# Layer norm of the last four batches on a turned x: rows through DRAM instead of transposes on TensorE

## The chip, the cores and the metric

The kernel runs on one NeuronCore of a Trainium2 chip. The metric is the device time of one execution in microseconds, the median of several runs. The engines are named as the profile names them: PE is TensorE's matmuls and PEld its weight loads, DVE is VectorE, ACT is ScalarE, POOL is GpSimd, SP is SyncE, which here issues DMAs only.

## The reference

Eight batches of 256 tokens with 256 features pass through two residual blocks. `ctx` has 120 rows of 256 per batch; the weights of the second block are ternary (-1, 0, 1) with a scale per output.

```python
def reference(x, ctx, w1_w, w1_s, w2_w, w2_s, h1_w, h1_s, h2_w, h2_s, w3_w, w3_s):
    n = layernorm(x)                                   # over the 256 features
    s = einsum('eth,efh->etf', n, ctx)
    x = x + einsum('etf,efh->eth', gelu_tanh(s) * s, ctx)
    n = layernorm(x)
    h = silu(tlin(n, w1_w, w1_s)) * tlin(n, w2_w, w2_s)     # 256 -> 1024
    h = gelu(tlin(h, h1_w, h1_s))                            # 1024 -> 1024
    h = gelu(tlin(h, h2_w, h2_s))                            # 1024 -> 1024
    return x + tlin(h, w3_w, w3_s)                           # 1024 -> 256
# tlin(x, w, s) = einsum('bsi,oi->bso', x, w) * s, layernorm without gain and bias, eps 1e-5
```

## The kernel before

Everything stays in float32 quality: each left operand of the large products is split into a rounded upper half (TH, half precision, written by ACT) and the rest (TL, written by VectorE), and TensorE multiplies both. The 1024x1024 layers are cut in 512x512 blocks and done with seven block products instead of eight (`ORDER`, `SUMS`, `PLAIN`), with the sums of blocks made on VectorE.

The work goes in two halves `c` of four batches, and in each half in tiles `t` of two batches (512 tokens). For each half: layer one of tile 2c (`layer1`), two block products, layer one of tile 2c+1, the other products of the first square layer (`late_products`), the second square layer (`square`, products s = 0 to 6), then layer four for its two tiles (`layer4_upper`, `layer4_lower`; half 1 first, then half 0), and `last` adds the result to x. The order on every engine is written out by hand; engines meet by semaphores, and each engine, SP too, does its list strictly in order.

The attention block of a batch is small and is tucked into the gaps of the large work: `stats` (mean and variance of x by VectorE into `mv`), `rstd` (POOL raises the variance to the power -0.5 into `rs`), `scale` (VectorE, line 894: xn = (x - mean) * power, two operations of 128 tokens each), `turn` (TensorE, line 1324: four transposes of 128x128 into a PSUM bank, `side(b)`), `copy_t` (ACT, line 612: the bank into `xt`), `score` (line 1335: two matmuls against ctx), `act_s` (gelu), `gate` (VectorE), `weigh` (line 1343), `resid` and the second layer norm, `turn(1, b)`, `first` and `second` into X, the operand of layer one. Batches 0 to 3 are done before and during the first layer one. Batches 4 and 5 are done at the end of the first half: VectorE scales them in `square(0)`, at s = 3 and s = 5; TensorE turns both after the first four products of layer four's half 1 (`attend4`) and scores them after the lower ones. Batches 6 and 7 are scaled, turned and scored inside `layer1(2)`.

Beside this runs a check of the weights' values: SP loads pieces of them into the spare buffers SL and Y, `xn[0]` and `xt` (`load_check`; each waits for the test before last), ACT takes the magnitude (`magnitude`, line 603) and VectorE tests (`test`, line 1036). Loads 7 and 8 are tested in `square(0)` at s = 5 and s = 6. POOL issues the weight loads (queue q0 in the profile), SP all others (queue q1).

In `square(0)` at s = 5 VectorE adds totals, tests, makes the low halves for product 6 (`lo`) and scales batch 5. At s = 6 it makes the totals of block (0, 0) (`total`, line 1030). On each of these waits ACT's gelu (line 714), on that ACT's rounded copy `hi4` (line 680), and on that layer four's first products on TensorE (line 1492) and VectorE's `lo4` (line 1000). Between the third copy and the fourth gelu stands the magnitude of load 8.

## Time and profile before

| | |
|---|---|
| median of 3 runs | 321.61 us (321.39 to 322.7) |
| profiled execution | 322.71 us, of which the span is 320.9 us |
| granted TensorE clock, every slice | 9 tenths or more of full speed; mean 1.0 |
| PE / DVE / ACT / POOL busy | 98% / 82% / 69% / 19% |
| the chain that ended last | PE 96% |
| queue q0 (POOL): packets, MB, share of 16 DMA engines | 21984, 52.43, 58.4% |
| queue q1 (SP): packets, MB, share | 9744, 22.11, 20.4% |

Busy time is the share of the span in which the engine had an instruction running. The chain is followed back from the last instruction, at each step to what released it; what stands in it sets the end. A row of a timeline gives the start in microseconds from the span's start, the duration of the merged instructions, the engine and the line, and in brackets how long the engine stood idle before and who released it. Rows named SPq or POOLq are the issuing of DMAs, not the transfer. A packet is one piece that a DMA engine moved.

### The profile page before, as it was taken

The page shows a single profiled execution, that of the slowest core. Times are in us where ns is not written, and L with a number is a line of the kernel's source. Part 1 is how long each engine was busy: PE and PEld are TensorE (multiplying, and loading weights), DVE is VectorE, ACT ScalarE, POOL GpSimd, SP SyncE. Part 2 cuts the span into 40 slices and gives each one's busy share as a digit, 9 for nine tenths or more (in the row PEclk, how much of TensorE's full clock was granted, in tenths as well). Part 3 has the DMA queues.
Part 4 walks back from the last instruction along what each step waited for, and adds up shares of the span by engine and source line. Part 5 has one row for each costly group of instructions (what it writes and reads, how often), then busy time and mean ns, then how long its engine had stood idle before and what let it go on. Part 6 is the DMA issues. An engine that isn't in the chain of part 4 may idle for free.

```text
span 320.9 us, 4928 instructions
## 1 busy us (share of the span) xinstructions
PE 313.8 (98%) x1624; PEld 226.9 (71%) x1624; DVE 264.2 (82%) x500; ACT 221.3 (69%) x372; POOL 59.6 (19%) x98
## 2 busy tenths in 40 slices
PE   7899999999999999999999999999999999999994
PEld 5799768774756657577898866876574756657693
DVE  4776996897996999998789494499899998998494
ACT  3657856781987857869825565978588975968740
POOL 5455010411120124114030003001121110220000
PEclk9999999999999999999999999999999999999999
DMA  7799999999999989998417055347599977877003
GB/s 205 253 173 270 207 262 319 315 393 400 321 340 419 303 294 254 334 270 187 133 66 262 2 196 194 137 129 261 198 275 293 394 254 293 203 189 198 0 29 111
DMA packets 31757, 74.90 MB, mean 233 GB/s; under 512 B 2160, under 2 KB 14192, under 8 KB 29296
## 3 DMA queue, kind: packets, MB, share of 16 engines
q0 software_dynamic: 21984, 52.43, 58.4%
q1 hardware_dynamic: 9744, 22.11, 20.4%
q8 instruction: 15, 0.25, 0.3%
q14 instruction: 14, 0.11, 0.1%
HBM read 71.39 MB, written 6.29 MB: 242 GB/s over the span
## 4 chain that ended last, share of the span: by engine, by line
PE 96%; DVE 1%; DMA 1%; POOL 0%; issue 0%; ACT 0%; DVEq 0%; POOLq 0%
PE P L1419 32%; PE P L1413 30%; PE P L1371 18%; PE P L1505 5%; PE P L1492 4%; PE P L1343 2%; PE P L1335 2%; PE P L1324 2%; DMA xs<-in_x 1%; PE P L1581 0%; POOL rs L474 0%; PE P L1588 0%; PE P L1574 0%; DVE st L900 0%; DVE hh L937 0%
## 5 line engine op out<-in xcount | busy, mean ns | idle before, releaser
L1419 PE MATMUL P<-TL,WR 128*128 128x512 f32 x448 | 107.4, 396 | 0.0
L1413 PE MATMUL P<-TH,WB 128*128 128x512 f16 x448 | 99.8, 379 | 0.0
L1419 PEld LDWEIGHTS P<-TL,WR 128*128 128x128 f32 x448 | 83.9, 188 | 18.6 <-DMA WR<-in_h 0.2
L673 ACT ACTIVATE TH<-H 128x512 f16<-128x512 f32 x112 | 67.9, 625 | 22.3 <-DVE H L986 14.0
L1413 PEld LDWEIGHTS P<-TH,WB 128*128 128x128 bf16 x448 | 42.4, 98 | 53.1 <-issue 4.5
L993 DVE TENSOR_TENSOR TL<-H,TH 128x512 fp32r<-128x512 f32 x112 | 73.2, 684 | 7.7 <-ACT TH L673 5.6
L1371 PE MATMUL P<-X,W 128*128 128x512 f32 (+1 forms) x320 | 62.5, 351 | 0.0
L1371 PEld LDWEIGHTS P<-X,W 128*128 128x128 f32 x320 | 51.7, 189 | 7.6
L986 DVE TENSOR_TENSOR H<-H 128x512 f32<-128x512 f32 x64 | 41.8, 683 | 0.0
L964 DVE SCALAR_TENSOR_TENSOR H<-P,sc,SLY 128x512 f32<-128x512 f32 (+1 forms) x40 | 25.3, 637 | 18.2 <-PE P L1371 11.0
L694 ACT ACTIVATE H<-P 128x512 f32<-128x512 f32 x48 | 28.5, 594 | 14.8 <-DMA blocks_h<-H 6.5
L662 ACT ACTIVATE SLY<-P,sc 128x512 f32<-128x512 f32 (+1 forms) x40 | 24.1, 603 | 18.4 <-PE P L1371 15.3
L714 ACT ACTIVATE H<-H,sc 128x512 f32<-128x512 f32 x40 | 27.4, 712 | 6.6 <-DVE H L1030 6.6
L1030 DVE TENSOR_TENSOR H<-P,H 128x512 f32<-128x512 f32 x40 | 25.6, 681 | 1.6 <-PE P L1413 1.3
L524 POOL DMA_DIRECT2D WB<-blocks_h x16 | 8.7, 546 | 97.2 <-PE P L1413 81.6
L1000 DVE SCALAR_TENSOR_TENSOR TL<-H,TH 128x512 fp32r<-128x512 f32 x32 | 20.6, 684 | 7.5 <-ACT TH L680 6.7
L1036 DVE SCALAR_TENSOR_TENSOR SLY<-SLY 128x1024 f32<-128x1024 f32 x14 | 17.0, 1218 | 3.0 <-ACT SLY L603 3.0
L680 ACT ACTIVATE TH<-H 128x512 f16<-128x512 f32 x32 | 18.0, 619 | 0.4 <-PE P L1413 0.4
L1505 PE MATMUL P<-WR,TL 128*128 128x256 f32 x128 | 18.3, 290 | 0.0
L469 POOL TENSOR_TENSOR rs<-mv,mhalf 128x2 f32<-128x2 f32 x14 | 11.4, 814 | 36.8 <-DVE mv L884 36.6
L603 ACT ACTIVATE SLY<-SLY 128x1024 f32<-128x1024 f32 x14 | 14.5, 1050 | 3.1 <-DMA SLY<-in_w 1.9
L714 ACT ACTIVATE H<-P,sc 128x512 f32<-128x512 f32 x24 | 15.5, 681 | 1.5 <-PE P L1413 1.5
(93 smaller groups left out, 257.1 us busy)
## 6 DMA issues: line engine op xcount, KB each, us to landing
WR<-blocks_h POOLq DMA_DIRECT2D x16, 1024.0 KB, 6.6
WR<-in_h POOLq DMA_DIRECT2D x11, 1024.0 KB, 9.4
WB<-blocks_h POOLq DMA_DIRECT2D x16, 512.0 KB, 5.5
WB<-in_h POOLq DMA_DIRECT2D x12, 512.0 KB, 8.1
H<-in_h POOLq DMA_DIRECT2D x8, 512.0 KB, 15.6
blocks_h<-H SPq DMA_DIRECT2D x4, 1024.0 KB, 8.9
SLY<-in_h SPq DMA_DIRECT2D x8, 512.0 KB, 5.0
SLY<-in_w SPq DMA_DIRECT2D x6, 512.0 KB, 8.1
```

The source lines that it names most:

```text
L662: eng.activation(SL[:, g % 2, at], bank1(t, 2 * m, p)[:, at], ACT.Silu, scale=sc[:, m:m + 1]).then_inc(s_sl, 1)
L673: eng.activation(TH[:, f % RING, :], operand(c, L, s, kk), ACT.Copy).then_inc(s_hi, 1)
L694: eng.activation(tile(target(c, L), to, m), bank(c, L, s, m)[:, :], ACT.Copy).then_inc(s_sn, 1)
L714: eng.activation(to, src, ACT.Gelu, scale=sc[:, col:col + 1]).then_inc(s_ge, 1)
L964: eng.scalar_tensor_tensor(out=source(t // 2, 0)[:, m, t % 2, at], in0=bank1(t, 2 * m + 1, p)[:, at], scalar=sc[:, 8 + m:9 + m], in1=SL[:, ...
L986: eng.tensor_tensor(tile(src, to, kk), tile(src, one, kk), tile(src, two, kk), ALU.subtract).then_inc(s_td, 1)
L993: eng.tensor_tensor(TL[:, f % RING, :], operand(c, L, s, kk), TH[:, f % RING, :], ALU.subtract).then_inc(s_lo, 1)
L1030: eng.tensor_tensor(to, bank(c, L, s, m)[:, :], other, ALU.add).then_inc(s_cd, 1)
L1371: out_ = eng.matmul(bank1(t, i, p)[:, at], w, X[:, t % 2, h, k, at], start=(k == 0 and h == 0), stop=(k == 1 and h == 1))
L1413: return eng.matmul(bank(c, L, s, m)[:, :], WB[r % WRING][:, at:at + 128], TH[:, fill(c, L, s, kk) % RING, :], start=(not lower_first and ...
L1419: return eng.matmul(bank(c, L, s, m)[:, :], WR[r % WRING][:, at:at + 128], TL[:, fill(c, L, s, kk) % RING, :], start=(lower_first and s in ...
L1505: out_ = eng.matmul(out_bank(c, half, j), TL[:, f % RING, j * 128:(j + 1) * 128], WR[r % WRING][:, k * D:(k + 1) * D], start=False, stop=( ...
```

## The change

For batches 4 to 7 the first layer norm is done on x that lies turned (features on partitions). The host hands the kernel a second input, `x_turned`; SP loads a batch of it into `xt` (256 KB, `load_turned`). The mean and the power of two batches go from `mv` and `rs`, where a token is a partition, to an internal DRAM tensor `rows` (`rows_out`: two DMAs, each of 128 partitions with 4 single floats, written 4 bytes at a time). From there they come back for each batch as two rows of 256 floats on all 128 partitions, into `xn[0]` (`rows_in`, 256 KB). VectorE then does (x - mean) in `center` and times the power in `spread_out`, both in place in `xt`, 128x512 values each. TensorE's `turn(0, b)` and ACT's `copy_t` for these batches are gone, and VectorE's `scale(0, b)`. The mathematics is the same. `score` now holds the wait for the bank that `turn` held.

```diff
+        rows = nc.dram_tensor("rows_x", [2, NB, 2, 128], f32, kind="Internal").ap()
...
+            def load_turned(b):
+
+                eng.wait_ge(s_s, b - 1)
+                eng.dma_start(xt[:, b % 2, :, :], x_turned[:, b, :, :]).then_inc(s_xT[b], 16)
+
+            def rows_out(b):
+
+                eng.wait_ge(s_mv[0], b + 2)
+                eng.dma_start(rows[0, b:b + 2, :, :].rearrange("b j p -> p (b j)"),
+                              mv[:, 0, b % 4:b % 4 + 2, :, 0].rearrange("p b j -> p (b j)"),
+                              allow_slow_non_contiguous=True).then_inc(s_row, 16)
+                eng.wait_ge(s_rs[0], b + 2)
+                eng.dma_start(rows[1, b:b + 2, :, :].rearrange("b j p -> p (b j)"),
+                              rs[:, 0, b % 4:b % 4 + 2, :].rearrange("p b j -> p (b j)"),
+                              allow_slow_non_contiguous=True).then_inc(s_row, 16)
+
+            def rows_in(b):
+                if b < 6:
+                    eng.wait_ge(s_tr[0], b - 1)
+                else:
+                    eng.wait_ge(s_xt, b - 1)
+                eng.dma_start(xn[0][:, b % 2, :, :],
+                              rows[:, b:b + 1, :, :].rearrange("v b j p -> b v (j p)").broadcast_to([128, 2, TB])).then_inc(s_bc[b], 16)
...
-            for i in range(2, 9):
+            for i in range(2, 4):
                 load_check(i)
+            load_turned(4)
+            load_turned(5)
+            for i in range(4, 8):
+                load_check(i)
+            rows_out(4)
+            eng.wait_ge(s_row, 32)
+            rows_in(4)
+            rows_in(5)
+            load_check(8)
+            rows_out(6)
+            load_turned(6)
+            load_turned(7)
+            eng.wait_ge(s_row, 64)
+            rows_in(6)
+            rows_in(7)
...
-                    if t == 2 and m in (3, 4):
-                        copy_t(3 + m)
...
-                    if i >= 2:
-                        if c == 0:
-                            copy_t(2 + i)
-                        else:
-                            gelu(c, 1, (1, 0), i)
+                    if i >= 2 and c == 1:
+                        gelu(c, 1, (1, 0), i)
...
+            def center(b):
+
+                eng.wait_ge(s_xT[b], 16)
+                eng.wait_ge(s_bc[b], 16)
+                eng.tensor_tensor(xt[:, b % 2, :, :], xt[:, b % 2, :, :], xn[0][:, b % 2, 0:1, :].broadcast_to([128, 2, TB]),
+                                  ALU.subtract).then_inc(s_xm, 1)
+
+            def spread_out(b):
+                eng.wait_ge(s_xm, b - 3)
+                eng.tensor_tensor(xt[:, b % 2, :, :], xt[:, b % 2, :, :], xn[0][:, b % 2, 1:2, :].broadcast_to([128, 2, TB]),
+                                  ALU.mult).then_inc(s_xt, 1)
...
-                    if c == 0 and s == 3:
-                        scale(0, 4)
...
                     if c == 0 and s == 5:
-                        scale(0, 5)
+                        for b in (4, 5):
+                            center(b)
+                            spread_out(b)
...
-                    if t == 2 and m < 2:
-                        scale(0, 6 + m)
+                    if t == 2 and m < 4:
+                        (center, spread_out)[m % 2](6 + m // 2)
...
-                if norm == 0 and b in (4, 5):
-
-                    gelu_done(eng, 0, 1, b, 0)
...
             def score(b):
                 eng.wait_ge(s_cf[b // 2], 16)
+                if b in (4, 5):
+
+                    gelu_done(eng, 0, 1, b, 0)
...
-                if t == 2 and i in (6, 8):
-                    turn(0, 3 + i // 2)
...
-                if (half, k, upper) == (1, 3, True):
-                    turn(0, 4)
-                    turn(0, 5)
```

How the rows of instructions stand now is shown at two places; the line numbers of the changed kernel differ from those before. On SP, from the load of the last scales (s3b) to the first stores of results (out), before:

```order
L421 DMA s3b<-in_s 128x256
L386 DMA SLY<-in_w 128x1024 [waits s_fl] x2
L388 DMA SLY<-in_w 128x1024 [waits s_fl] x2
L391 DMA SLY<-in_h 128x1024 [waits s_fl] x3
L427 DMA out<-xs 128x512 [waits s_y2] x4
```

and now, with check load 8 on its own behind the rows:

```order
L449 DMA s3b<-in_s 128x256
L414 DMA SLY<-in_w 128x1024 [waits s_fl] x2
L381 DMA xt<-in_x_turned 128x512 [waits s_s] x2
L416 DMA SLY<-in_w 128x1024 [waits s_fl] x2
L419 DMA SLY<-in_h 128x1024 [waits s_fl] x2
L386 DMA rows_x<-mv 128x4x1 [waits s_mv1]
L390 DMA rows_x<-rs 128x4x1 [waits s_rs1]
L399 DMA xn<-rows_x 128x2x256 [waits s_tr1,s_row]
L399 DMA xn<-rows_x 128x2x256 [waits s_tr1]
L419 DMA SLY<-in_h 128x1024 [waits s_fl]
```

The writing of the rows stands behind check load 7 (the second of L419 x2), their reading behind the landing of both writes, and check load 8 behind the reading.

On VectorE, the end of s = 5 and the beginning of s = 6 of the second square layer, from the test of load 7 (SLY) over the low halves (TL) to the totals (H<-P), before:

```order
L1036 SCALAR_TENSOR_TENSOR SLY,fl<-SLY 128x1024 [waits s_ab]
L993 TENSOR_TENSOR TL<-H1,TH 128x512 [waits s_tf,s_hi] x4
L894 TENSOR_SCALAR xn0<-xs,mv,rs 128x256 [waits s_rs1,s_mv1,s_tr1]
L894 TENSOR_SCALAR xn0<-xs,mv,rs 128x256
L1030 TENSOR_TENSOR H0<-P6,H0 128x512 [waits s_sn,s_p]
L1030 TENSOR_TENSOR H0<-P7,H0 128x512 [waits s_sn,s_p]
L1000 SCALAR_TENSOR_TENSOR TL<-H0,TH 128x512 [waits s_tf,s_hi]
```

and now, with the same names:

```order
L1086 SCALAR_TENSOR_TENSOR SLY,fl<-SLY 128x1024 [waits s_ab]
L1043 TENSOR_TENSOR TL<-H1,TH 128x512 [waits s_tf,s_hi] x4
L939 TENSOR_TENSOR xt<-xt,xn0 128x512 [waits s_bc4,s_xT4]
L944 TENSOR_TENSOR xt<-xt,xn0 128x512 [waits s_xm]
L939 TENSOR_TENSOR xt<-xt,xn0 128x512 [waits s_bc5,s_xT5]
L944 TENSOR_TENSOR xt<-xt,xn0 128x512 [waits s_xm]
L1080 TENSOR_TENSOR H0<-P6,H0 128x512 [waits s_sn,s_p]
L1080 TENSOR_TENSOR H0<-P7,H0 128x512 [waits s_sn,s_p]
L1050 SCALAR_TENSOR_TENSOR TL<-H0,TH 128x512 [waits s_tf,s_hi]
```

Four operations that wait for DMAs (s_bc, s_xT) stand where two scalings stood, ahead of the totals.

## Rows read from the trace of the kernel before

**Rows 1.** The page, part 1: busy us, share of the span, instructions.

```profile
PE 313.8 (98%) x1624; PEld 226.9 (71%) x1624; DVE 264.2 (82%) x500; ACT 221.3 (69%) x372; POOL 59.6 (19%) x98
```

**Rows 2.** The chain of waits in order of time: start us, us, what.

```profile
137.08 7.28 PE P L1419 x32
...
147.83 1.75 PE P L1492 x16
149.58 0.87 PE P L1324 x8
...
174.11 0.44 PE P L1324 x4
...
176.41 0.44 PE P L1324 x4
```

**Rows 3.** DVE's timeline around 141 us: start, us, what, idle before and releaser.

```profile
137.98 2.49 DVE L993 TENSOR_TENSOR TL<-H,TH 128x512 fp32r<-128x512 f32 x4
140.39 0.72 DVE L894 TENSOR_SCALAR xn<-xs,mv,rs 128x256 f32<-128x256 f32 x2
141.04 1.28 DVE L1030 TENSOR_TENSOR H<-P,H 128x512 f32<-128x512 f32 x2
143.03 0.69 DVE L1000 SCALAR_TENSOR_TENSOR TL<-H,TH 128x512 fp32r<-128x512 f32 x1 [0.71 <-ACT TH L680]
```

**Rows 4.** ACT's timeline in the same stretch.

```profile
141.75 0.72 ACT L714 ACTIVATE H<-H,sc 128x512 f32<-128x512 f32 x1 [2.46 <-DVE H L1030]
...
145.50 1.04 ACT L603 ACTIVATE SLY<-SLY 128x1024 f32<-128x1024 f32 x1
...
147.06 0.61 ACT L680 ACTIVATE TH<-H 128x512 f16<-128x512 f32 x1
```

**Rows 5.** PE's timeline, first products of layer four.

```profile
147.67 1.91 PE L1492 MATMUL P<-WB,TH 128*128 128x256 bf16 x16
```

**Rows 6.** SP's timeline: two loads of check data, of one window each.

```profile
126.86 0.33 SPq L391 DMA_DIRECT2D SLY<-in_h  x1
...
131.22 0.33 SPq L391 DMA_DIRECT2D SLY<-in_h  x1
```

**Rows 7.** POOL's timeline: the power of batch 5.

```profile
120.27 1.04 POOL L469 TENSOR_TENSOR rs<-mv,mhalf 128x2 f32<-128x2 f32 x1 [5.96 <-DVE mv L884]
```

**Rows 8.** DMA queues, 127 to 130 us: packets, MB, share of 16 engines.

```profile
q0 software_dynamic: 593, 0.87, 123.0%
```

**Rows 9.** The same, 130.2 to 133 us.

```profile
q0 software_dynamic: 299, 0.41, 63.6%
q1 hardware_dynamic: 142, 0.52, 50.3%
```

**Rows 10.** The same, 134.3 to 136.6 us.

```profile
q1 hardware_dynamic: 141, 0.52, 57.6%
```

**Rows 11.** The same, 2.5 to 3 us and then 7 to 7.5 us.

```profile
q1 hardware_dynamic: 143, 0.13, 102.5%
...
q1 hardware_dynamic: 97, 0.04, 29.1%
```

**Rows 12.** DMA issues over the whole run: count, KB each, median us to landing.

```profile
xs<-in_x SPq DMA_DIRECT2D x2, 128.0 KB, 2.2
out<-xs SPq DMA_DIRECT2D x4, 128.0 KB, 2.6
```

**Rows 13.** DVE's timeline: a pair in which the second waits for the first.

```profile
167.23 0.68 DVE L1163 SCALAR_TENSOR_TENSOR SLY<-P,s3b 128x512 f32<-128x512 f32 x1
167.94 0.69 DVE L1168 TENSOR_TENSOR xs<-SLY,xs 128x512 f32<-128x512 f32 x1
```

**Rows 14.** DMA issues between 126.5 and 134 us: a weight load.

```profile
WR<-in_h POOLq DMA_DIRECT2D x1, 1024.0 KB, 10.6
```

**Rows 15.** DVE's timeline in the third layer-one stretch.

```profile
173.19 0.73 DVE L894 TENSOR_SCALAR xn<-xs,mv,rs 128x256 f32<-128x256 f32 x2
...
182.36 0.75 DVE L964 SCALAR_TENSOR_TENSOR H<-P,sc,SLY 128x512 f32<-128x512 f32 x1 [1.35 <-PE P L1371]
```

More of the change, by code:

```diff
@@ L48, with xattn_ffn @@
 SPIN = (13, 1)
-def xattn_ffn(nc, x, ctx_tok, ctx_feat, w12, h1, h2, w3, cols, s3, out):
+def xattn_ffn(nc, x, x_turned, ctx_tok, ctx_feat, w12, h1, h2, w3, cols, s3, out):
     f32, f32r, u16, i32 = mybir.dt.float32, mybir.dt.float32r, mybir.dt.uint16, mybir.dt.int32
@@ L162, in xattn_ffn @@
         s_m4, s_y, s_y2, s_out = sem("s_m4"), sem("s_y"), sem("s_y2"), sem("s_out")
+        s_xT = {b: sem(f"s_xT{b}") for b in range(4, NB)}
+        s_bc = {b: sem(f"s_bc{b}") for b in range(4, NB)}
+        s_row, s_xm = sem("s_row"), sem("s_xm")
         s_ab, s_fl, s_fp, s_ft = sem("s_ab"), sem("s_fl"), sem("s_fp"), sem("s_ft")
@@ L1690, in _ @@
                     out_.then_inc(g_m3, 1)
-_INS = ["x", "ctx_tok", "ctx_feat", "w12", "h1", "h2", "w3", "cols", "s3"]
+_INS = ["x", "x_turned", "ctx_tok", "ctx_feat", "w12", "h1", "h2", "w3", "cols", "s3"]
 def kernel(x, ctx_1024, L0_ffn_w1_w, L0_ffn_w1_s, L0_ffn_w2_w, L0_ffn_w2_s, L0_ffn_h1_w, L0_ffn_h1_s,
@@ L1714 @@
         "x": np.asarray(x).reshape(NB * TB, D),
+        "x_turned": np.asarray(x).reshape(NB, 128, 2, 2, 128).transpose(4, 0, 3, 2, 1).reshape(128, NB, 2, TB),
         "ctx_tok": np.pad(c.transpose(1, 0, 2), ((0, 128 - S), (0, 0), (0, 0))),
```

## The prediction

> **What bounds the kernel now.** I read the page first, then the chain of waits, then the timelines of the stretch where the change lands, then the DMA queues there. TensorE is busy 313.8 of 320.9 us [rows 1], and the chain that ended last is TensorE almost from end to end. So only two things move the time: work taken off TensorE, and a wait put in front of it. The transposes that the change removes stand in that chain three times: one piece of 8 for batches 4 and 5, and two of 4 for batches 6 and 7 [rows 2]. The granted clock is full in every slice of the page, so it takes no part in the sum.
>
> **What goes from TensorE.** 16 transposes in pieces of 0.87, 0.44 and 0.44 us [rows 2]: 1.75 us. The chain counts by how much each piece holds up the next matmul, so this is the term. This is the whole possible gain, 0.54% of the run.
>
> **What goes from and comes to the other engines.** ACT loses four copies out of the PSUM bank, all in places where it is not the last to be ready. VectorE loses four pairs of scalings of about 0.72 us (one is at 140.39 in [rows 3]) and gets eight operations on 128x512 values. The nearest row is a 128x512 tensor_tensor: four in a row start 0.60 us apart (137.98 to 140.39) [rows 3], and one that waits for the one before it starts 0.71 us after it [rows 13]. A batch therefore costs 1.31 us. Batches 6 and 7 pay this between the gates of the third layer-one stretch, where VectorE has its scaling at 173.19 and sits idle 1.35 us before 182.36 [rows 15]. The extra there is 2 x (1.31 - 0.72) = 1.2 us, which this idle time swallows; without that cover it would cost up to 1.2.
>
> **The place that decides: VectorE before layer four.** Before, the scaling of batch 5 ran at 140.39 and the totals of the last block began at 141.04 [rows 3]. Everything behind is a tight relay: gelu on ACT at 141.75, a magnitude of 1.04 us between, the fourth rounded copy at 147.06 lasting 0.61 [rows 4]. VectorE itself waits 0.71 us for ACT in it at 143.03 [rows 3]. So the fourth copy is ready 147.67 - 141.04 = 6.63 us after the totals begin. TensorE starts layer four at 147.67 [rows 5] and takes 1.75 us for 16 products of four copies [rows 2], so it wants the fourth copy at 147.67 + 3/4 x 1.75 = 148.98. The totals may then begin at 142.35 and no later; every later microsecond is a microsecond of TensorE, because all engines in this relay are in order.
>
> In the changed order VectorE has center(4), spread_out(4), center(5), spread_out(5) ahead of the totals. With all data there they start at 140.39, 141.10, 141.70 and 142.41, and the totals at 143.01: 0.66 us of stall even in the best case. If the rows of batch 5 land at T, the totals begin at T + 1.31 and the stall is T - 141.04. The changed order queues behind the waiting instruction all of VectorE: totals, the low halves for layer four, the test of data 8, the statistics of batch 7; ACT and TensorE wait for the first two.
>
> **When do the rows land?** SP is in order too. It issues the check load 7 at 126.86 [rows 6] and only then rows_out(4). The power of batch 5 is ready at 121.31 [rows 7], so values are no limit, the place in SP's queue is. I follow the queue:
>
> The check load issued at 126.86 moves nothing before 130.2: from 127 to 130 only POOL's queue q0 has packets [rows 8]. The next one, issued at 131.22 [rows 6], moves from 134.3 [rows 10]. So an SP transfer begins 3.1 to 3.3 us after its issue while POOL loads weights. The first is through at 133.0 (142 packets in [rows 9]: one packet for each 4 KB row of a partition, 128, and the completions).
>
> Writing the rows: two DMAs of 128 partitions x 4 single floats. Packets here go one per contiguous piece, so I count 1024 packets, 64 on each of 16 engines. No row shows a 4-byte packet. From below, the smallest packets that do show (97, on average 0.4 KB, 29.1% of 0.5 us) [rows 11] take 0.291 x 16 x 0.5 / 97 = 24 ns: 1.5 us. From above, each also waits for a packet of POOL's, 1.23 x 16 x 3 / 593 = 100 ns [rows 8]: 64 x 0.124 = 7.9 us. In [rows 9] the two queues did run mixed, so neither end is excluded; I take 5.0, near the middle: 138.0. A write lands 0.4 us later than a load of that size (2.6 against 2.2) [rows 12]; with SP's wake-up I take 0.7: 138.7.
>
> The Trainium skill (DMA: Bandwidth & Descriptors, Rules for kernel authors) says that a strided last dimension is lowered to one descriptor per element. The count of rows above does not rest on it, but it speaks against this edit: a packet per partition instead would make the writes 64 / 4 = 16 packets an engine, at most 2.0 us, and T some 3 us earlier. No run so far shows a strided write of this kind.
>
> Reading them back: two loads of 256 KB as 512 packets of 1 KB. They begin 3.2 us after issue as above: 141.9. A 1 KB packet takes 1.025 x 16 x 0.5 / 143 = 57 ns [rows 11]: 32 x 57 = 1.8 us alone, 32 x 157 = 5.0 us with a POOL packet each; I take 3.4: 145.3, and 0.5 for the completion: T = 145.8. Ends: all low, and the load starting as in a quiet stretch, 133.0 + 1.5 + 0.4 + 2.2 [rows 12] + 1.4 for the 384 packets beyond 128 = 138.5, which is in time; all high, 133.0 + 7.9 + 0.7 + 3.3 + 5.0 + 0.5 = 150.4.
>
> **Sum.** Stall 145.8 - 141.0 = 4.8; transposes -1.75; net +3.0 us. The profiled execution took 322.71 us, 320.9 of it the span and 1.8 around it; it would become 325.7. It was 1.1 above the median of 321.61, which becomes 324.6, my forecast. By the ends of T: 0.66 - 1.75 = -1.1 (320.5) and 9.4 - 1.75 = +7.6 (329.2).
>
> **Edits at nothing.** The turned x of batches 4 and 5 is issued after check 3, some 40 us ahead of its use; those of 6 and 7 and their rows, free to start some 5 us after layer four's first products at 147.67 [rows 5], have until 173 [rows 15], 20 us where the chain above needs 19 with a check load at its head (126.9 to 145.8); that is the thinnest cover of the four, and each microsecond over it would stop VectorE between two gates. Check load 8 now goes behind the rows, needs the 2.8 us of [rows 9] after T, and its magnitude stands 4.5 us after the totals begin (145.50 against 141.04) [rows 3, 4], T + 5.8: covered, and if not, it would stop ACT ahead of the fourth copy, microsecond for microsecond. The weight load that POOL issued near 126.8 landed after 10.6 us [rows 14], near 137.5, and is used half-way through the 32 products of 137.08 [rows 2], at 140.7; small packets mixed with its tail may push it 1 to 2 us: covered.
>
> **Rivals.** (1) Pure gain: the relay has slack I do not see and the rows are early; 321.61 - 1.75 = 319.9. For it: TensorE alone is the bound [rows 1]. Against it: 0.66 us of added VectorE work in a relay with 1.3 us of room, and SP's queue. Chance 0.07. (2) The rows land in time (T below 141.7), the gain shrinks by 0.66: 320.5, no change that can be measured. It needs the low end of both packet prices and no 3 us delay. Chance 0.18. (3) The forecast's mechanism with a price far above: the float writes go at the pace that q1's packets had in [rows 9], 142 in 2.8 us, 51 per us, so 1024 take 20 us; then T is 153 + 9.5 = 162.5, the stall 21, the time 341. It ends slower as well; 0.08. (4) The wait on the rows in place of the transposes, as summed: slower from T = 144.4 on, where the stall exceeds 1.75 + 1.6. This is my forecast, 0.67, of which 0.07 falls under that point; its own range is 322.4 to 329.2.
>
> **Chances.** A change of 0.5%, 1.6 us, is about what a measurement of this kernel can tell from none. Faster 0.07; same 0.18 + 0.07 = 0.25; slower 0.60 + 0.08 = 0.68. The range 320.2 to 331 leaves out the pure gain and the crawl, 0.15 in all, and a little of each neighbour.
>
> **What the profile after would show.** Right: no transposes between the 16 products of layer four and the next ones; VectorE idle for several microseconds before the first center, released by DMA; the totals starting at 143 to 149; TensorE idle in its first layer-four products, waiting for ACT's copy; q1 with about a thousand packets under 512 B near 133 to 139. Wrong: VectorE's center at 140.4 without idle time, or many fewer packets (the floats are merged), or the transposes of layer four worth more than 0.87 us. A second stall at the scores of batches 6 and 7 would break the part on cover.

## The result and the profile after

| | before | changed |
|---|---|---|
| median | 322.01 us (321.39 to 322.86, 6 runs) | 353.24 us (352.44 to 354.91, 6 runs) |
| profiled execution, its span | 322.71, 320.9 us | 354.44, 352.6 us |
| mean granted clock | 1.0 | 0.959 |

The ratio is 1.0975 (95% interval 1.0954 to 1.0997): 9.7% slower. The direction and the place were forecast; the size (+3.0 us) was short by a factor of ten. Of the versions below, the one with the writes alone was profiled in a slow execution (336.31 us; the three fast ones took 329.74, 329.82 and 330.82), so its time is read from those three and its trace only for where TensorE stops.

Three more rows of the kernel before: its DMA counts, then the groups of the lower products and of layer four's upper products (busy, mean ns | idle before).

```profile
DMA packets 31757, 74.90 MB, mean 233 GB/s; under 512 B 2160, under 2 KB 14192, under 8 KB 29296
...
L1419 PE MATMUL P<-TL,WR 128*128 128x512 f32 x448 | 107.4, 396 | 0.0
...
L1492 PE MATMUL P<-WB,TH 128*128 128x256 bf16 x128 | 15.9, 273 | 0.0
```

The page of the changed kernel: busy time by engine, then the granted TensorE clock by slice, the DMA counts and queues, and the same two groups of instructions (busy, mean ns | idle before, who ended it).

```profile
PE 321.9 (91%) x1608; PEld 231.0 (66%) x1608; DVE 267.1 (76%) x500; ACT 219.6 (62%) x368; POOL 59.3 (17%) x98
...
PEclk9999999999999999787599699999999999999998
...
DMA packets 35533, 77.01 MB, mean 218 GB/s; under 512 B 4400, under 2 KB 17456, under 8 KB 33072
...
q1 hardware_dynamic: 13520, 24.21, 26.9%
...
L1469 PE MATMUL P<-TL,WR 128*128 128x512 f32 x448 | 109.3, 400 | 8.6 <-DMA WR<-in_h 8.5
...
L1542 PE MATMUL P<-WB,TH 128*128 128x256 bf16 x128 | 18.1, 291 | 9.5 <-ACT TH L723 9.4
```

Against [rows 1] TensorE does 16 instructions fewer, is busy 8.1 us longer and is idle 23.6 us longer. Three things are to be seen. The clock row has slices at 5 to 8 tenths, where before every slice had 9. The lower products (L1469) wait 8.5 us for a weight load and layer four (L1542) 9.4 us for ACT's copies; both groups had no idle time before. And q1 has 13520 - 9744 = 3776 packets more: 2048 single floats, 1024 pieces of 1 KB of rows, 512 pieces of the turned x, and 16 completions for each of 12 DMAs. Of those, 2240 are under 512 bytes (4400 against 2160), the floats and the completions. The floats are not merged.

TensorE's timeline in the changed kernel, only its stops from 140 us on:

```profile
149.89 5.28 PE L1469 MATMUL P<-TL,WR 128*128 128x512 f32 x16 [8.54 <-DMA WR<-in_h]
...
166.54 2.12 PE L1542 MATMUL P<-WB,TH 128*128 128x256 bf16 x8 [7.91 <-ACT TH L723]
169.10 1.04 PE L1542 MATMUL P<-WB,TH 128*128 128x256 bf16 x4 [0.44 <-ACT TH L723]
171.18 1.03 PE L1542 MATMUL P<-WB,TH 128*128 128x256 bf16 x4 [1.04 <-ACT TH L723]
...
189.95 0.65 PE L1371 MATMUL P<-ident,xn 128*128 128x128 f32 x3 [1.20 <-issue]
195.30 1.23 PE L1371 MATMUL P<-ident,xn 128*128 128x128 f32 x5 [4.70 <-issue]
```

SP's timeline (what it issues; a gap is a wait) and below it VectorE's before layer four:

```profile
127.14 0.33 SPq L419 DMA_DIRECT2D SLY<-in_h  x1
127.51 0.44 SPq L386 DMA_DIRECT2D rows_x<-mv  x1
127.99 0.58 SPq L390 DMA_DIRECT2D rows_x<-rs  x1
150.82 1.39 SPq L399 DMA_DIRECT2D xn<-rows_x  x2
...
175.10 0.36 SPq L390 DMA_DIRECT2D rows_x<-rs  x1
...
195.21 1.08 SPq L399 DMA_DIRECT2D xn<-rows_x  x2
```

```profile
160.71 0.69 DVE L939 TENSOR_TENSOR xt<-xt,xn 128x512 f32<-128x512 f32 x1 [20.78 <-DMA xn<-rows_x]
...
163.15 0.69 DVE L939 TENSOR_TENSOR xt<-xt,xn 128x512 f32<-128x512 f32 x1 [1.02 <-DMA xn<-rows_x]
...
164.48 1.28 DVE L1080 TENSOR_TENSOR H<-P,H 128x512 f32<-128x512 f32 x2
```

The totals that began at 141.04 [rows 3] begin at 164.48, because 4 KB of rows took 22.8 us from the second write's issue (127.99) to the issue of the read (150.82), and the read another 10 to 12. The second pair of writes, which starts while POOL's queue is silent, takes 20.1 us as well (175.10 to 195.21).

Answers of the DMA view (packets, MB, share of 16 engines): q1 from 174 to 177 us, q0 from 141 to 151 us, q0 in the same stretch of the version without writes (below), q1 from 181 to 194 us; then the weight load that POOL issued between 126.5 and 134 us (KB, us to landing).

```profile
q1 hardware_dynamic: 1056, 0.00, 16.8%
```

```profile
q0 software_dynamic: 41, 0.17, 85.0%
```

```profile
q0 software_dynamic: 1339, 2.74, 100.9%
```

```profile
q1 hardware_dynamic: 92, 0.18, 101.2%
```

```profile
WR<-in_h POOLq DMA_DIRECT2D x1, 1024.0 KB, 22.4
```

The first row is the surprise. The 1024 floats of the second pair (and 32 completions) are off the engines within 3 us, at 0.168 x 16 x 3 / 1056 = 7.6 ns each, but their DMAs are complete only at 195.2. The first pair, which shares the engines with POOL's loads, is slower there: of its 1056 packets 44 are moved before 133 us and the other 1012 between 133 and 141, with engine time of 0.742 x 16 x 8 / 1012 = 94 ns each. Its DMAs are complete at 150.8, still 10 us after the last packet.

In that time whatever else is in flight crawls. From 141 to 151 us 4 KB packets of POOL's take 0.85 x 16 x 10 / 41 = 3.3 us each: 41 in 10 us, where the version without writes has 1339. In the second stretch SP's loads of the turned x still have 144 packets from 178 to 180 us, and then 92 in the 13 us from 181 to 194. The weight load of [rows 14] goes from 10.6 to 22.4 us.

Sum for the profiled execution: weight load 8.54, ACT's copies 7.91 + 0.44 + 1.04 = 9.39, the two stops before the transposes of the second layer norm 5.90: 23.8 of idle time. TensorE's busy time without the 1.75 us of transposes would be 312.05; it is 321.9, so slower instructions cost 9.85 (8.8 if the 313.1 us of the version without writes, whose clock is 1.0, are the measure). 23.8 + 9.85 - 1.75 = 31.9, against 31.7 of span. The slower instructions stand behind the stops. The windows show it (us; busy and count of PE, PEld, DVE, ACT, POOL; granted clock, DMA share, GB/s):

```profile
137.00:141.00 4.00, 4.00 (x20) 3.10 (x17) 2.92 (x6) 2.03 (x4) 0.75 (x1) 1.00 1.96 47
141.00:150.00 9.00, 0.47 (x3) 0.11 (x1) 0.00 (x0) 0.00 (x0) 0.75 (x1) 0.77 0.85 16
150.00:158.00 8.00, 8.00 (x30) 5.19 (x31) 0.00 (x0) 0.00 (x0) 0.00 (x0) 0.83 0.86 208
...
166.00:178.00 12.00, 9.91 (x43) 7.38 (x44) 8.75 (x17) 10.98 (x19) 1.05 (x1) 0.56 0.50 123
...
195.00:204.00 9.00, 8.70 (x38) 7.90 (x38) 7.36 (x12) 3.97 (x6) 1.12 (x2) 0.69 0.39 95
```

The clock is 1.00 until TensorE stops at 141. It is 0.83 from 150 to 158, behind the first stop, and 0.56 from 166 to 178, behind the second: over those 12 us on average near the lower of its two levels (1.2 of 2.4 GHz). Behind the third, from 195 to 204, it is 0.69.

### The profile page after: what moved, and what is told of

It is laid out like the page before. It is cut to its first block, busy times and chain, and to the rows that moved or that the text cites. A ratio compares the mean times of both kernels' runs of the same rounds, so it can differ in the third digit from the quotient of the medians.

```text
span 352.6 us, 4898 instructions
## 1 busy us (share of the span) xinstructions
PE 321.9 (91%) x1608; PEld 231.0 (66%) x1608; DVE 267.1 (76%) x500; ACT 219.6 (62%) x368; POOL 59.3 (17%) x98
## 3 DMA queue, kind: packets, MB, share of 16 engines
q1 hardware_dynamic: 13520, 24.21, 26.9%
## 4 chain that ended last, share of the span: by engine, by line
PE 74%; DMA 12%; issue 4%; ACT 4%; DVE 4%; SPq 0%; DVEq 0%; ACTq 0%
PE P L1469 21%; PE P L1463 20%; PE P L1421 17%; DMA rows_x<-rs 6%; PE P L1555 5%; PE P L1542 4%; DMA xn<-rows_x 3%; DMA SLY<-in_w 2%; PE P L1385 2%; PE P L1393 2%; DVE H L1036 2%; ACT TH L716 2%; PE P L1371 2%; ACT SLY L646 1%; PE P L1564 1%
## 5 line engine op out<-in xcount | busy, mean ns | idle before, releaser
L1469 PE MATMUL P<-TL,WR 128*128 128x512 f32 x448 | 109.3, 400 | 8.6 <-DMA WR<-in_h 8.5
L1469 PEld LDWEIGHTS P<-TL,WR 128*128 128x128 f32 x448 | 84.8, 190 | 28.2 <-DMA WR<-in_h 9.4
L716 ACT ACTIVATE TH<-H 128x512 f16<-128x512 f32 x112 | 67.9, 624 | 20.1 <-DVE H L1036 13.7
L1542 PE MATMUL P<-WB,TH 128*128 128x256 bf16 x128 | 18.1, 291 | 9.5 <-ACT TH L723 9.4
L1555 PE MATMUL P<-WR,TL 128*128 128x256 f32 x128 | 21.5, 325 | 0.0
L1542 PEld LDWEIGHTS P<-WB,TH 128*128 128x128 f16 x128 | 12.0, 102 | 13.6 <-issue 8.4
L1555 PEld LDWEIGHTS P<-WR,TL 128*128 128x128 f32 x128 | 19.2, 225 | 0.2
L939 DVE TENSOR_TENSOR xt<-xt,xn 128x512 f32<-128x512 f32 x4 | 2.7, 687 | 21.8 <-DMA xn<-rows_x 21.8
```

Of the source, the lines that this page charges most:

```text
L716: eng.activation(TH[:, f % RING, :], operand(c, L, s, kk), ACT.Copy).then_inc(s_hi, 1)
L1469: return eng.matmul(bank(c, L, s, m)[:, :], WR[r % WRING][:, at:at + 128], TL[:, fill(c, L, s, kk) % RING, :], start=(lower_first and s in ...
L1542: out_ = eng.matmul(out_bank(c, half, j), TH[:, f % RING, j * 128:(j + 1) * 128], WB[r % WRING][:, k * D:(k + 1) * D], start=(k == 0 and ( ...
L1555: out_ = eng.matmul(out_bank(c, half, j), TL[:, f % RING, j * 128:(j + 1) * 128], WR[r % WRING][:, k * D:(k + 1) * D], start=False, stop=( ...
```

## The experiments

The kernel before ran beside every group: 321.95, 321.79, 321.73 and 321.76 us median. Theory W is that the single-float writes are the loss, by the wait for them and by what they do to other transfers.

**1. Nothing is written** (e1_no_write). The rows are loaded from x, in the same pieces.

```diff
-            rows_out(4)
-            eng.wait_ge(s_row, 32)
...
-            rows_out(6)
...
-            eng.wait_ge(s_row, 64)
...
-   rows[:, b:b + 1, :, :].rearrange("v b j p -> b v (j p)").broadcast_to([128, 2, TB])
+   x[2 * b:2 * b + 2, :].rearrange("(b v) p -> b v p", b=1).broadcast_to([128, 2, TB])
```

> The changed kernel without the writes of mean and power to DRAM: the two rows come back from two rows of the input x, so the first layer norm of batches 4 to 7 uses wrong numbers. Theory W (the single-float writes are the cost: they finish about 22 us after their issue and hold up all other transfers meanwhile): without them no wait on the rows, no late weight load and no stall later; time near 321, at most 1.5 us either side of the kernel before. Rival R (the broadcast reads of the same two rows are a cost of their own: 12 us from issue to landing in the changed kernel): VectorE waits for them before its first center until 140 to 146 us, time 322 to 327.

320.24 us (320.02 to 321.46), ratio 0.9948 (0.9932 to 0.9964), clock 1.0. VectorE, no wait:

```profile
139.74 0.69 DVE L935 TENSOR_TENSOR xt<-xt,xn 128x512 f32<-128x512 f32 x1
...
142.40 1.28 DVE L1076 TENSOR_TENSOR H<-P,H 128x512 f32<-128x512 f32 x2
```

So turned loads, read-back, VectorE's eight operations and the missing transposes together are a gain of 1.7 us. All of the loss hangs on the writes and on the waits for them; rival R (the broadcast reads cost by themselves) falls. It also corrects a term: center begins at 139.74, not at 140.39, since the scaling of batch 4, 0.65 us at s = 3, is gone too, and TensorE does not wait at layer four.

**2. The writes alone** (e2_write_only). The kernel before, transposes and all, with the four writes on SP and nobody waiting for them until the end.

```diff
-            for i in range(2, 9):
-                load_check(i)
+            for i in range(2, 8):
+                load_check(i)
+            rows_out(4)
+            load_check(8)
+            rows_out(6)
```

> The kernel before, with its transposes, plus only the four single-float writes at the places where the changed kernel has them on SP; nobody waits for them before the end. Theory W, with writes that hold up other transfers: the weight load for the last product of the second square layer comes about 8.5 us late, the clock is lower for a while (1.5 to 3 us), and the turning for the second layer norm stops for 5 to 6 us; time 335 to 339. Rival Q (the writes only take long by themselves, and all of the cost is the waiting for them in SP and VectorE): time 322 to 323.

329.82 us (329.74 to 330.82), ratio 1.0245 (1.0212 to 1.0279). TensorE's first stop:

```profile
149.24 3.35 PE L1436 MATMUL P<-TL,WR 128*128 128x512 f32 x7 [8.17 <-DMA WR<-in_h]
```

Writes that nobody waits for cost 7.9 us, and the trace shows through what: another engine's weight load. So about a quarter of the 31 us is clogging alone. Rival Q (322 to 323) falls, but theory W's own range for this run, 335 to 339, was 5 us too high: the stop of 5 to 6 us at the second layer norm did not come. TensorE does these transposes at 175.49 without a stop marked "issue", though the DMA engines then move only 48 GB/s (166 to 178 us). What is left of the 31 us is the wait for the rows, the second pair's stretch in the changed order, and the clock.

**3. Each float in 512 bytes of its own** (e3_spread). The same 1024 writes of 4 bytes per pair, read back from x.

```diff
-        rows = nc.dram_tensor("rows_x", [2, NB, 2, 128], f32, kind="Internal").ap()
+        rows = nc.dram_tensor("rows_x", [2, NB, 2, 128, 128], f32, kind="Internal").ap()
...
-                eng.dma_start(rows[0, b:b + 2, :, :].rearrange("b j p -> p (b j)"),
+                eng.dma_start(rows[0, b:b + 2, :, :, 0].rearrange("b j p -> p (b j)"),
```

> The changed kernel with each float written to its own 512 bytes of DRAM (1024 writes as before, over 512 KB instead of 4 KB), and the rows read back from two rows of the input x, so the numbers are wrong. If the writes are slow because they all fall into the same few lines of DRAM and queue there: they finish within 3 to 6 us, and the time is 321 to 326. If each single-float write has its price wherever it goes: they finish about 22 us after issue as in the changed kernel, time 348 to 354 (a little less if the read back from x is quicker).

326.96 us (326.86 to 329.6), ratio 1.0173 (1.0109 to 1.0238). SP's and VectorE's timelines:

```profile
127.25 0.43 SPq L386 DMA_DIRECT2D rows_x<-mv  x1
...
136.51 0.96 SPq L399 DMA_DIRECT2D xn<-in_x  x2
```

```profile
144.54 0.69 DVE L939 TENSOR_TENSOR xt<-xt,xn 128x512 f32<-128x512 f32 x1 [4.87 <-DMA xn<-in_x]
```

9.3 us instead of 23.3 from the first write's issue to the read, no late weight load (9.2 us), a wait of 4.87 us. That is somewhat more than the 3 to 6 us and the 321 to 326 us expected. The number and size of the writes are those of the changed kernel; what makes the crawl is that they lie close together. This version behaves as I had forecast for the changed one.

**4. Half of the floats** (e4_half, partitions 0 to 63, `mv[0:64, ...]` and `rs[0:64, ...]`, read from x), and later **the means alone** (e8_means_only, without the second DMA of `rows_out`).

> The changed kernel with only the floats of partitions 0 to 63 written (512 instead of 1024 for a pair of batches, still four DMAs); the other tokens' mean and power are wrong. If the price is per write: the first pair is done about 9 to 11 us earlier, near 140 us, and VectorE's stall before center shrinks from 20.8 us to about 11; with the weight load less late as well the time is 334 to 343. If the price is per DMA and not per write: no change, 352 to 354.

341.61 us (339.76 to 341.89), ratio 1.0586 (1.0535 to 1.0636). SP:

```profile
127.42 0.69 SPq L386 DMA_DIRECT2D rows_x<-mv  x1
...
149.84 1.34 SPq L399 DMA_DIRECT2D xn<-in_x  x2
...
171.85 0.58 SPq L390 DMA_DIRECT2D rows_x<-rs  x1
...
186.09 0.80 SPq L399 DMA_DIRECT2D xn<-in_x  x2
```

> The changed kernel without the write of the power: 512 floats per pair of batches instead of 1024, still dense, 16 in each 64 bytes; rows read from x, so the values are wrong. Theory N (price per write): 10 us of crawl after about 3 us, rows_in issued near 140, center of batch 4 near 149, stall about 8, total 330 to 335 us. Theory D64 (price by depth, pieces served side by side): the crawl stays near 20 us, rows_in at 148 to 150, total 340 to 350, as where half the partitions were written (341.61).

332.13 us (331.37 to 332.4), ratio 1.0311 (1.0289 to 1.0333), rows_in at 141.58, center of batch 4 at 150.25 after 10.35 us of waiting. Both leave 512 floats with 16 in each 64 bytes, and they differ: 14.2 and 9.4 us from the last write's issue to the read in the second pair. With half the partitions the total lies in the expected 334 to 343, but not for the expected reason: the first pair was to be done 9 to 11 us earlier, and the read leaves at 149.84 against 150.82. The means alone come out as theory N (a price for each write) has it. The price is neither one for a float nor one for the depth of a piece alone.

**5. How close is too close** (e5_own64, e9_own16, e11_own8, e10_by_partition). As 3 with 64, 16 and 8 bytes for each float; in the last the 8 floats of a partition stand together without gaps, and 128 partitions in a row.

```diff
-        rows = nc.dram_tensor("rows_x", [2, NB, 2, 128], f32, kind="Internal").ap()
+        rows = nc.dram_tensor("rows_x", [2, NB, 2, 128, 16], f32, kind="Internal").ap()   # own64; 4, 2: own16, own8
+        rows = nc.dram_tensor("rows_x", [NB // 2, 128, 4, 2], f32, kind="Internal").ap()  # by_partition
```

> The changed kernel with each float of mean and power written into 64 bytes of its own (1024 writes of 4 bytes as before, 8 in each 512 bytes instead of 128); the rows that are read back are taken from x, so the values are wrong, the bytes and places of the reading are as before. Theory D64 (what costs is the number of writes that fall into one piece of 64 bytes, 16 in the changed kernel, 1 here): like the run with 512 bytes of its own, writes over 8 to 10 us after issue, rows read at 136 to 138, total 326 to 328 us. Theory D512 (the same with pieces of 512 bytes, 128 there, 8 here, price in proportion to the depth): 20 x 8 / 128 = 1.3 us more than with 512 bytes of its own, 327 to 329, hardly to be told apart. Theory F (only a stride of at least 512 bytes helps, since each smaller write reads and rewrites a piece shared with others, one after another): still a crawl of 10 us or more, 340 us and over.

> The same with each float in 16 bytes of its own: 1024 writes of 4 bytes, 4 in each 64 bytes, 32 in each 512 bytes. Theory D64, price in proportion to the depth: 20 x 4 / 16 = 5 us of writing beyond the spread case's own, rows read near 138 to 141, total 328 to 333. Theory D512: 20 x 32 / 128 = 5 us, the same. Theory N (every write that is not alone in its piece costs the same, about 20 ns): 20 us again, writes done near 150, total near 350.

> The changed kernel with each float in 8 bytes of its own: 1024 writes of 4 bytes, 8 in each 64 bytes, from 8 neighbouring partitions (16 in the changed kernel, 4 with 16 bytes each). What is read back comes from x, so the values are wrong. Theory D, in proportion from 4 writes (10.5 us from issue to rows_in) to 16 (22.8): about 14.6, rows_in near 142, total 332 to 338. Theory S, if an engine serves 8 neighbouring partitions and so owns its 64 bytes: still 10 to 11 us, total 328 to 330. If S holds with another division among the engines, the crawl comes back in part and this run can't tell it from D; then the run with the floats by partition decides.

> The changed kernel with the same 1024 writes of 4 bytes into the same 4 KB, without gaps in the end, but the 8 floats of a partition stand together in 32 bytes instead of 512 bytes apart (each still written by itself; what is read back comes from x, so the values are wrong). Each 64 bytes get 16 writes as in the changed kernel, but from 2 partitions instead of 16. Theory D (it is the number of writes into one piece of memory that costs): a crawl of 20 us, rows_in issued near 150, total 340 to 350. Theory S (it is that many partitions, and so several DMA engines, write into the same piece at once): rows_in issued near 138, as with 16 bytes for each float (138.36), total 327 to 331.

All of 3 to 5 side by side. "First" is the time from the first write's issue to the read's issue in the first pair, "second" from the last write's issue to the read's in the second pair, where POOL's queue is silent; a value with "up to" is one where SP reached the read no earlier for another reason.

| version | floats per pair | in each 64 bytes | first | second | median (ratio, interval) |
|---|---|---|---|---|---|
| changed | 1024 | 16 | 23.3 | 20.1 | 353.24 (1.0975) |
| half the partitions | 512 | 16 | 22.4 | 14.2 | 341.61 (1.0586) |
| means alone | 512 | 16 | 14.1 | 9.4 | 332.13 (1.0311) |
| by partition | 1024 | 16, of 2 partitions, 8 by each DMA | 14.1 | 7.2 | 332.43 (1.0362, 1.0323 to 1.0401) |
| 8 bytes each | 1024 | 8 | 14.0 | 6.7 | 332.05 (1.0313, 1.0292 to 1.0335) |
| 16 bytes each | 1024 | 4 | 11.0 | up to 3.2 | 329.26 (1.0221, 1.0192 to 1.0249) |
| 64 bytes each | 1024 | 1 | 9.9 | up to 2.9 | 326.63 (1.013, 1.0104 to 1.0157) |
| 512 bytes each | 1024 | 1 | 9.3 | up to 3.1 | 326.96 (1.0173) |

Two rows of SP's timeline in the by-partition version, behind its 7.2:

```profile
163.84 0.52 SPq L390 DMA_DIRECT2D rows_x<-rs  x1
...
171.01 0.80 SPq L399 DMA_DIRECT2D xn<-in_x  x2
```

The price falls with the density: 20 us, 7 us, and with 16 bytes each a rest that the totals still show against 64 bytes (329.26 to 326.63, intervals apart; the interval of 512 bytes each overlaps both). 64 bytes each are as good as 512. Theory F (only 512 bytes help) is refuted. Theory N (every write alike) fits the means alone (332.13, in its range) and is refuted by 16 bytes each. Theory D64 (the depth of a piece alone, pieces served side by side) is refuted by the means alone: half the writes at the same depth take half the time. Theory S (many partitions in one piece) fails too: by it the by-partition version would be as quick as 16 bytes each (327 to 331), and 8 bytes each would take 328 to 330.

The by-partition version does not refute a price by density. Its 332.43 us lie in neither expected range, but its 16 floats in each 64 bytes come from two DMAs, 8 by each, while in the changed kernel one DMA writes all 16. Counted for each DMA it has the density of 8 bytes each, and it costs the same: 7.2 against 6.7 us, 332.43 against 332.05. That they come from 2 partitions there and from 8 here makes no difference. So these runs show that the number of writes counts and that their density within one DMA counts, more than in proportion (from 16 to 8 the 20.1 us fall to 6.7). The size of the piece is not shown: theory D512 expected 327 to 329 for 64 bytes each and can't be told from D64. Why half the partitions cost more than half the values is open as well; nobody tested how many DMA engines write into one piece. The second-pair times are from one profile each.

**6. The same dense writes, asked for earlier** (e13_floats_early).

```diff
-                    if c == 0 and s in (2, 3):
-                        stats(0, 2 + s)
+                    if c == 0 and s in (1, 2):
+                        stats(0, 3 + s)
...
-            for i in range(4, 8):
+            for i in range(4, 7):
                 load_check(i)
             rows_out(4)
+            load_check(7)
```

> The changed kernel with its single-float writes for batches 4 and 5 asked for one product earlier: statistics one product earlier, both writes behind check load 6 (issued near 120.3) and ahead of check load 7. Nothing is left out and the writes are the same 1024 dense ones. It tells what of the loss is the place in the order and what the writes themselves. Theory W (the writes clog whatever is in flight, wherever they stand): rows written only at 141 to 144 (20 to 22 us after issue), rows_in there, center of batch 4 at 146 to 150, check load 7 landing in the crawl, near 144 instead of 133, so ACT's magnitude of data 7 waits some 10 us and the lower products of the fifth block with it; the weight loads issued at 121 to 127 late too. Total 340 to 356 us, no clear gain over the changed kernel (353.24). Rival P (the place was the trouble: asked for early, the rows are there in time for 139.8 and the rest is covered): 325 to 335, about the cost of clogging alone (330.32).

346.68 us (345.57 to 347.66), ratio 1.0755 (1.0708 to 1.0802). SP, ACT and TensorE:

```profile
120.91 0.44 SPq L386 DMA_DIRECT2D rows_x<-mv  x1
...
127.23 0.34 SPq L419 DMA_DIRECT2D SLY<-in_h  x1
148.61 1.08 SPq L399 DMA_DIRECT2D xn<-rows_x  x2
```

```profile
150.57 1.06 ACT L647 ACTIVATE SLY<-SLY 128x1024 f32<-128x1024 f32 x1 [18.61 <-DMA SLY<-in_h]
```

```profile
154.88 6.22 PE L1470 MATMUL P<-TL,WR 128*128 128x512 f32 x16 [7.66 <-DMA WR<-in_h]
```

Asked for 6.6 us earlier, the rows are there 2.2 us earlier (the read leaves at 148.6, where 141 to 144 was expected), and check load 7, which had landed before the crawl, is now caught in it and stops ACT for 18.6 us. The place in the queue is not what was wrong: theory W holds (340 to 356), rival P (325 to 335) falls.

**7. A version without single floats** (e7_rows_turned, then e12_rows_early). Mean, variance and power of batches 4 to 7 share a 128x32 piece; VectorE turns it in 32x32 blocks, and a pair's rows leave as 32 pieces of 128 bytes. The second version makes the statistics one product earlier. Both compute the whole reference.

```diff
+            def turn_stats(k):
+                eng.wait_ge(s_rs[0], 6 + 2 * k)
+                eng.transpose(sT[:, k, :], sA[:, :]).then_inc(s_sT, 1)
...
+            def rows_out(b):
+                k = b // 2 - 2
+                eng.wait_ge(s_sT, k + 1)
+                for i in range(4):
+                    eng.dma_start(rows[k].rearrange("v b j p -> (v b j) p")[:, 32 * i:32 * i + 32],
+                                  sT[32 * i + 16 * k:32 * i + 16 * k + 16:2, k, :]).then_inc(s_row, 16)
...
-            for i in range(4, 8):
+            for i in range(4, 7):
                 load_check(i)
             rows_out(4)
+            load_check(7)
-            eng.wait_ge(s_row, 32)
+            eng.wait_ge(s_row, 64)
```

> A version meant to beat both: mean and power of batches 4 to 7 lie in one 128x32 piece, VectorE turns it in 32x32 blocks (two operations of some 0.1 us), and a pair's rows go out as 32 pieces of 128 bytes (4 DMAs of 8) instead of 1024 single floats; the writes are issued right behind the turning, ahead of check load 7. Nothing is left out. Theory W (the single floats alone were the loss): rows written by 131, read back by 137 to 138, center of batch 4 at about 139.8 without a wait, all as in the run without writes: 320.2 to 321.0 us, ratio 0.995 to 0.997 to the kernel before. Rival Q (the queue on SP still brings the rows late, the loads wait for POOL's packets): rows at 141 to 144, a stall of 1 to 4 us, 321.5 to 325. Rival M (any write from SBUF of less than 512 bytes clogs as before): over 330.

321.16 us (320.73 to 322.27), ratio 0.998 (0.9959 to 1.0001), just above theory W's 320.2 to 321.0; rival M (over 330) falls. ACT waits longer for check load 7, and VectorE is late for the totals:

```profile
134.64 1.06 ACT L653 ACTIVATE SLY<-SLY 128x1024 f32<-128x1024 f32 x1 [2.85 <-DMA SLY<-in_h]
```

```profile
142.92 1.28 DVE L1092 TENSOR_TENSOR H<-P,H 128x512 f32<-128x512 f32 x2
```

> The version with the rows turned on VectorE, with the statistics of batches 4 and 5 one product earlier and the turning at the place where the statistics of batch 5 stood (about 119.3). Its four writes leave SP behind check load 6 and are done before 126.9, check load 7 goes out at 126.9 instead of 128.4, and the rows are asked for right behind it. Nothing is left out. Theory L (the version before lost 0.5 us because four DMA issues held check load 7 up by 1.5 us, ACT's magnitude waited 0.87 longer, and the totals before layer four began at 142.92, 0.57 after the latest time of 142.35): ACT's magnitude back at 133.8, center of batch 4 at 139.8, totals at 142.5, no wait at layer four, span 318.4 to 318.6, time 320.2 to 320.7, ratio 0.994 to 0.997. Rival (any DMA work of the rows costs in another place, such as POOL's weight loads): 321.0 or more, as the version before (321.16).

320.26 us (320.13 to 321.55), ratio 0.9962 (0.9946 to 0.9978), as expected: a gain of 0.4%, small but with its interval clear of 1, over the kernel before. SP, and VectorE without a wait:

```profile
120.66 2.70 SPq L394 DMA_DIRECT2D rows_x<-sT  x4
127.06 0.34 SPq L422 DMA_DIRECT2D SLY<-in_h  x1
128.00 0.90 SPq L402 DMA_DIRECT2D xn<-rows_x  x2
```

```profile
120.18 0.20 DVE L945 STREAM_TRANSPOSE sT<-sA 128x32 f32<-128x32 f32 x1
...
139.77 0.68 DVE L951 TENSOR_TENSOR xt<-xt,xn 128x512 f32<-128x512 f32 x1
...
142.42 1.28 DVE L1092 TENSOR_TENSOR H<-P,H 128x512 f32<-128x512 f32 x2
```

The same bytes, 4 KB per pair, in 32 pieces instead of 1024, and the gain of the missing transposes is there: 1.2 us by the ratio, 1.5 by the medians.

## Why the prediction was wrong in size

**The writes, the step that failed.** The text priced 1024 floats as packets, "24 ns" from below and "64 x 0.124 = 7.9 us" from above, and took 5.0 us, from 133.0 to 138.0. As packets the first pair's took 8 us (133 to 141), the upper end; the second pair's, alone on the engines, took 7.6 ns each, below the lower end. But the DMA is complete 20.1 to 22.8 us after its issue, 10 to 19 us after the last packet. The forecast had 0.7 us for that part. It took this from a write of 128 KB [rows 12], and both packet prices from other transfers, none of which writes single floats side by side. With the floats 512 bytes apart the forecast's own numbers nearly hold: read issued at 136.5 (forecast 138.7), layer four's stops 4.2 us in sum (forecast 4.8), a time of 326.96 (forecast 324.6). The rest of that difference is in TensorE's busy time, 315.5 us against the 312.05 that the forecast implies, at a mean clock of 0.99.

**The rival that had it.** "The float writes go at the pace ... 51 per us, so 1024 take 20 us" gave T = 162.5 and 341 us, at 0.08. Batch 5's rows were used at 163.15: T was right to 0.7 us, by luck: the floats did not go at that pace, the first pair's left the engines in 8 us and the second's in 3. Its time was 12 us short, because it too counted the wait alone.

**Edits at nothing, the second failure.** The weight load of [rows 14], "may push it 1 to 2 us: covered", landed after 22.4 us instead of 10.6 and stopped TensorE for 8.54; in the writes-alone version the same stop is 8.17. A slow transfer was priced by who waits for it, never by what else it slows. For batches 6 and 7 the text gave "20 us where the chain above needs 19": VectorE never waited for those rows (the two waits in its group are those of batches 4 and 5). But their writes fall into the stretch of 176 to 195, and there TensorE stops 1.20 and 4.70 us, marked "issue". The stop is 5.9 us in the changed kernel, 2.1 with the writes asked for earlier, 1.2 (0.9 and 0.3) with half the partitions, none in the versions with a crawl under 10 us, and none with the writes alone, where the same dense writes are in flight. Late loading of instructions, whose queue q8 has 15 packets in the page after, could be the cause, but no run took that alone. The cause of these 5.9 us stays open.

**The clock.** "It takes no part in the sum" was true of before and fell with the stops: 9.85 us of slower instructions. None of my cases had a price for it, though all but the pure gain had a stall.

**What held.** The queue on SP: check load 7 landed 6.3 us after its issue at 127.14, at 133.4 (forecast 133.0). One packet for each float: in the Trainium skill, DMA: Bandwidth & Descriptors, Rules for kernel authors, a strided last dimension becomes one descriptor per element; the 2048 extra packets agree. The same page (Specifications) says that transfers under 512 bytes are read-modify-writes in the DMA engine. By that alone floats at 64 or at 512 bytes each should be as bad as dense ones, since each is still written 4 bytes at a time; they cost 326.63 and 326.96 against 353.24 us, so here the rule doesn't tell the cases apart, the density does. The transposes: 1.75 us forecast, 1.7 measured without the writes. The relay from totals to layer four: the latest start was put at 142.35; totals at 142.40 and 142.42 give no wait, those at 142.92 one of 0.4 us on TensorE. The 0.66 us of stall in the best case was wrong, by the scaling of batch 4 that I had counted as removed but not as time given back.

## What to carry to other kernels

Do not write single floats next to each other into DRAM from many partitions: turn them on chip first (0.2 us on VectorE for a 128x32 piece) so that they leave in pieces, here of 128 bytes. Leaving 64 bytes to each takes the crawl away too, but it is the poorer way: that version was still 1.3% slower than the kernel before, and it did not read its values back. Price a transfer of an unseen kind not only by its own length and by who waits for it, but by everything that is in flight beside it. And where a stall on TensorE is possible, give the slower clock behind it a price as well; here slower instructions cost 9.85 us behind 23.8 us of stops.

## What the runs showed that I had not expected

- 1024 writes of 4 bytes into 4 KB of DRAM leave the DMA engines in 3 us when nothing else is in flight and are complete after 20. The packets in the DMA view don't show the end; the time at which the waiting SP goes on does.
- Meanwhile the 4 KB packets of POOL's queue take 3.3 us each, and the core moves 17 GB/s instead of 275.
- Half of the partitions cost more (14.2 us) than the means alone (9.4 us), with equally many floats.
- After the second stop (7.91 us) TensorE's granted clock was 0.56 over the next 12 us.
